# Row numbers loaded four at a time, row loads three quads ahead, early sums regrouped in DRAM, z rows by plain gathers

## The chip, the cores and the metric

The kernel runs on one core of a Trainium2 chip. The core has TensorE (PE), VectorE (DVE), ScalarE (ACT), GpSimd (POOL) and SyncE (SP). Of these SP, ACT and POOL issue transfers here, and all transfers share 16 DMA engines. The metric is the device time of one execution in microseconds (us); lower is better.

## The reference, cut to what matters

```python
N, E, D, F = 12500, 212500, 256, 128
h = relu(layernorm(x))                                # (N, D)
in_deg  = min(segment_sum(1, dst, N), 511)
out_deg = min(segment_sum(1, src, N), 511)
sum3d   = segment_sum(edge_attr @ W_sum + b_sum, src, N)   # edge_attr is (E, F)
cent = sigmoid(centralities @ W_cent + b_cent)
vor  = sigmoid(voronoi_values @ W_vor + b_vor)
out = x + h + z_in[in_deg] + z_out[out_deg] + cent + vor + sum3d
```

The edges come in order of `dst`, and the heavy part is the sum over `src`, which is random. Everything is float32.

## The kernel before, in words

Node `100 a + w` belongs to window `w` (100 windows) and lies on partition `a` (125 partitions). A tile is 128 edges, a quad four tiles; there are 416 quads, cut into four segments of 25, 175, 130 and 86 quads. Within a segment the kernel sorts edge rows by window with a counting sort into DRAM, then reads the sorted rows back and adds them up.

The sort, for quad `q` (all engines run one loop over quads, each with its own written order of instructions):

- SP loads edge rows into `edge_ring`, six slots of five tiles (L354 to L359). A slot is refilled when its scatters have landed; SP asks for that at quad `q` for scatters of about quad `q - 4` (`LOAD_AHEAD`, L384 to L386).
- DVE makes the one-hot tile `hot_w` of the next quad (L517), PE ranks it against running counts (`rank`, L870), ACT reduces the ranks to positions (`positions`, L762) and writes each edge's key behind its row (`row_keys`, L769), PE adds the quad to the counts (`rebase`, L876 and L877, behind the quad's pieces in PE's order), and DVE turns positions into indices (`index`, L703, the last thing of its quad). `INDEX_RING` is 12 quads deep: DVE waits for the scatters of quad `q - 12`.
- POOL scatters each tile's 128 rows of 520 bytes to the segment's area in DRAM (L427), one indirect DMA a tile.

A segment's sorted rows are read back during the next segment, in pieces of 256 rows, one window each: 150, 450, 360 and 270 pieces (one piece for each 256 rows and one for each window). For piece `n`: its issuer waits for slot `n % 11` of `piece_ring`, reads the row number from `row_i` into a register (L343, a TENSOR_LOAD, then FUSED_REGOPS and SEQ_ASSERT for the bounds) and issues the load of 130 KB (L344, with one FUSED_REGOPS and one MOVE ahead); DVE makes the one-hot matrix `hot_n` (L585); PE multiplies (L886, four matmul records, two row groups of two passes); DVE folds the product onto the sum of the window so far in `stage` (L608), six stages of two pieces; ACT stores two pieces' sums at a time to `sums` in DRAM (L777). `sums` has 125 partitions, 1230 pieces and 129 numbers (128 sums and the count). `last_i` tells which piece holds a window's whole sum.

A planner at the head (L110 to L164) lays out `side[q]`, the list of side work of quad `q` that every engine walks: it spreads the pieces of the segment before evenly over the quads from `quad0[s] + LAG` (`LAG = INDEX_RING + 2`) to four quads before the segment's end, and puts node work (sigmoids, layernorm, ACT and DVE), histogram work for the in-degrees and others where a cost table leaves room under `BUDGET`. In the main loop SP issues a quad's piece loads at that quad (L391 to L393), behind its edge load.

The last segment's 270 pieces come behind the main loop, in one loop over `c` on each engine. SP loads the even pieces, ACT the odd ones (ten ahead). POOL gathers the z_in rows of all windows into `base` with an accumulating indirect DMA (L434). From `c = 170 + 10` on, window `w = c - 180` is finished: four rows of `sums`, one for each segment, are loaded into `table_ring` (six slots; SP the first two segments, ACT the other two; for each one register read at L330 and one load at L331, 63 KB in 125 partitions of 516 bytes); four steps later DVE adds the four counts (L676), makes `out_i` (L678), adds count times b_sum (L683), POOL gathers the z_out row with accumulation (L434), PE transposes and adds the four tables (L897, eight matmul records), ACT copies (L791), PE multiplies by W_sum (L907), and DVE adds to `base` (L689). SP stores `base` to the output behind its loop (L403).

## Time and profile before

| What | us |
|---|---|
| median of 3 runs | 3323.89 |
| lowest and highest run | 3298.01, 3340.47 |
| the profiled execution's own time | 3312.39 |
| its span in the trace | 3310.5 |

```profile
PE 2012.2 (61%) x9285; PEld 1456.0 (44%) x9285; DVE 1798.8 (54%) x5794; ACT 762.6 (23%) x3965; POOL 2067.2 (62%) x1869
```

The line gives each engine's busy time, its share of the span and its instructions. PEld is TensorE's load of weights. SP has no row, as it only issues. The page cuts the span in 40 slices of 83 us, a digit being tenths:

```profile
PE   6546766776443366676666636666665666466664
DVE  8646677777346556666666645454544445233331
POOL 4777777777777776566666674444446885344443
PEclk8656666666555577777777657667776556677786
DMA  3346644544554377777777647677775997555558
```

PEclk is the granted TensorE clock in tenths of full speed, DMA the mean busy share of the 16 DMA engines. Times in the text are from the span's start. An engine name with q behind it (SPq, ACTq) is the engine's queue: waits, register work and issues of transfers.

### The profile page before, as it was taken

Reading aid. Unit: us, or ns where it says so; the run is one execution under the profiler, and the core shown is the slowest. Engines: PE = TensorE matmul, PEld = TensorE weight load, DVE = VectorE, ACT = ScalarE, POOL = GpSimd, SP = SyncE. Lnnn points to the kernel's source line nnn. Section 1 sums busy time; section 2 is a strip of 40 time slices with the busy share of each in tenths; the row PEclk is TensorE's granted clock in tenths of the full one; section 3 lists DMA queues with packets and bytes.
Section 4 is the critical chain, followed back from the end, with each engine's and each line's share of the span. In section 5 each row is a group of like instructions: output and inputs, shape, how many; then the busy total and the mean of one; then the engine's idle time right before and its main releaser. Section 6 shows DMA issues by size and latency. Waiting matters only on the chain.

```text
span 3310.5 us, 47321 instructions
## 1 busy us (share of the span) xinstructions
PE 2012.2 (61%) x9285; PEld 1456.0 (44%) x9285; DVE 1798.8 (54%) x5794; ACT 762.6 (23%) x3965; POOL 2067.2 (62%) x1869
## 2 busy tenths in 40 slices
PE   6546766776443366676666636666665666466664
PEld 2235544444221045455555415555553555455553
DVE  8646677777346556666666645454544445233331
ACT  2222322222245422222233341111111000000000
POOL 4777777777777776566666674444446885344443
PEclk8656666666555577777777657667776556677786
DMA  3346644544554377777777647677775997555558
GB/s 106 102 142 195 186 135 133 140 136 133 145 143 122 103 204 203 201 209 207 207 216 214 184 127 192 187 192 191 195 196 154 188 187 174 130 123 130 128 129 212
DMA packets 671281, 546.20 MB, mean 165 GB/s; under 512 B 116444, under 2 KB 639549, under 8 KB 670990
## 3 DMA queue, kind: packets, MB, share of 16 engines
q1 hardware_dynamic: 409188, 296.29, 33.3%
q0 software_dynamic: 136352, 136.66, 17.9%
q10 hardware_dynamic: 125450, 110.23, 11.1%
q8 instruction: 78, 1.28, 0.2%
q14 instruction: 213, 1.74, 0.2%
HBM read 339.32 MB, written 203.17 MB: 164 GB/s over the span
## 4 chain that ended last, share of the span: by engine, by line
DMA 27%; POOL 24%; issue 13%; PE 12%; SPq 9%; ACTq 7%; DVE 6%; ACT 1%; DVEq 0%; POOLq 0%
POOL sorted L427 24%; DMA piece_ring<-sorted 24%; PE bank L886 9%; SPq L343 5%; ACTq L330 3%; DVE hot_n L585 2%; ACTq L331 2%; SPq L344 2%; DMA sums<-stage 1%; PE bank L897 1%; DMA sorted<-edge_ring,pos_i 1%; ACTq L343 1%; PE bank L907 1%; DVE gate L646 1%; SPq L357 0%
## 5 line engine op out<-in xcount | busy, mean ns | idle before, releaser
L427 POOL DMA_INDIRECT sorted<-edge_ring,pos_i x1660 | 1664.9, 1003 | 880.0 <-issue 449.8
L886 PE MATMUL bank<-piece_ring,hot_n 128*125 128x129 f32 x4920 | 1120.3, 385 | 863.3 <-DVE hot_n L585 859.3
L886 PEld LDWEIGHTS bank<-piece_ring,hot_n 128*125 128x125 f32 x4920 | 932.1, 272 | 1127.1 <-DVE hot_n L585 1104.2
L585 DVE SCALAR_TENSOR_TENSOR hot_n<-bank,wkey,piece_ring 128x250 f32<-128x250 f32 x1230 | 583.7, 475 | 1180.6 <-DMA piece_ring<-sorted 1139.3
L762 ACT ACTIVATE junk<-bank,mark_col 128x100 bf16<-128x100 f32 x1664 | 549.7, 342 | 1401.9 <-PE bank L870 1386.9
L608 DVE SCALAR_TENSOR_TENSOR stage<-stage,same,bank 125x129 f32<-125x129 f32 x1226 | 417.4, 340 | 106.1 <-DMA sums<-stage 91.1
L434 POOL DMA_INDIRECT base<-in_L_gnn_z_out_dram,out_i x100 | 199.5, 1995 | 305.2 <-DVE base L689 213.5
L762 ACT ACTIVATION_READ_ACCUMULATOR junk<-bank,mark_col 128x1 f32 x1664 | 337.4, 203 | 0.0
L876 PE MATMUL bank<-hot_w,after_b 128*128 128x400 bf16 x416 | 192.2, 462 | 171.5 <-ACT junk L762 171.5
L913 PE MATMUL bank<-hot_dl,hot_dh 128*125 128x100 bf16 x1661 | 224.9, 285 | 36.6 <-DVE hot_dh L517 36.1
L913 PEld LDWEIGHTS bank<-hot_dl,hot_dh 128*125 128x125 bf16 x1661 | 186.4, 191 | 86.7 <-DVE hot_dh L517 69.3
L434 POOL DMA_INDIRECT base<-in_L_gnn_z_in_dram,deg_i x100 | 199.4, 1994 | 30.6 <-issue 30.6
L870 PE MATMUL bank<-hot_w,before_b 128*128 128x400 bf16 x416 | 191.1, 459 | 4.5 <-DVE hot_w L517 4.5
L791 ACT ACTIVATE sumT<-bank 128x125 f32<-128x125 f32 x100 | 27.6, 277 | 720.1 <-DVE stage L608 311.0
L877 PE MATMUL bank<-hot_w,unmark_b 128*128 128x400 bf16 x416 | 193.0, 464 | 0.0
L841 PE MATMUL bank<-hot_t,ones_b 128*128 128x400 bf16 x416 | 155.3, 417 | 46.0 <-DVE hot_t L517 45.5
L907 PE MATMUL bank<-w_sb,sumT 128*125 128x256 f32 x200 | 91.2, 547 | 131.8 <-ACT sumT L791 116.0
L517 DVE TENSOR_TENSOR hot_dh<-dst_parts,iota_h 128x500 bf16<-128x500 bf16 x416 | 171.1, 411 | 0.0
L517 DVE TENSOR_TENSOR hot_w<-src_w,iota_h 128x400 bf16<-128x400 bf16 x416 | 148.7, 358 | 0.0
L876 PEld LDWEIGHTS bank<-hot_w,after_b 128*128 128x128 bf16 x416 | 53.9, 130 | 213.1 <-ACT junk L762 212.3
L897 PEld LDWEIGHTS bank<-ident,edge_ring 125*128 125x128 f32 x800 | 142.7, 251 | 10.6
L517 DVE TENSOR_TENSOR hot_dl<-dst_parts,iota_h 128x400 bf16<-128x400 bf16 x416 | 147.3, 354 | 0.1
(102 smaller groups left out, 1247.6 us busy)
## 6 DMA issues: line engine op xcount, KB each, us to landing
piece_ring<-sorted SPq DMA_DIRECT2D x1095, 130.0 KB, 3.9
edge_ring<-in_edge_attr_dram SPq DMA_DIRECT2D x332, 320.0 KB, 3.8
sums<-stage ACTq DMA_DIRECT2D x615, 126.0 KB
sorted<-edge_ring,pos_i POOLq DMA_INDIRECT x1660
piece_ring<-sorted ACTq DMA_DIRECT2D x135, 130.0 KB, 6.4
edge_ring<-sums SPq DMA_DIRECT2D x200, 63.0 KB
edge_ring<-sums ACTq DMA_DIRECT2D x200, 63.0 KB
base<-in_x_dram SPq DMA_DIRECT2D x20, 560.0 KB
```

The source lines that it names most:

```text
L343: row = eng.value_load(row_i[32 * (s % 2):32 * (s % 2) + 1, c:c + 1], min_val=0, max_val=edges_in[s])
L427: g.indirect_dma_start(rows, bass.IndirectOffsetOnAxis(index, 0), edge_ring[:, slot, at, :], None).then_inc(s_scatter[slot], 16)
L434: g.indirect_dma_start(base[0:NODE_P, w, :], None, table[:, :], bass.IndirectOffsetOnAxis(index[0:NODE_P, w:w + 1], 0), compute_op=ALU.add ...
L517: return v.tensor_tensor(to, part.unsqueeze(2).to_broadcast([P, 2, n, 2]), iota_h[:, 0:n, :].unsqueeze(1).to_broadcast([P, 2, n, 2]), ALU. ...
L585: v.scalar_tensor_tensor(out=hot_n[:, n % HOT_SLOTS, 0:G, :], in0=iota_ps.unsqueeze(1).to_broadcast([P, G, LOC]), scalar=wkey[:, s % 2, c: ...
L608: v.scalar_tensor_tensor(out=to, in0=stage[0:LOC, (n - 1) // STAGE % STAGES, (n - 1) % STAGE, :], scalar=same[0:LOC, s % 2, c:c + 1], in1=new,
L762: last = a.activation(junk[:, t, :], part[:, t // 2, :, t % 2], ACT.Relu, bias=mark_col[:, :], accum_out=pos_f[:, q % 4, t:t + 1])
L870: t_.matmul(ps_rank, before_b[:, :], hot, start=False, stop=True, skip_group_check=True).then_inc(s_rank, 1)
L876: t_.matmul(ps_rank, after_b[:, :], hot, start=False, stop=False, skip_group_check=True)
L877: t_.matmul(ps_rank, unmark_b[:, :], hot, start=False, stop=True, skip_group_check=True).then_inc(s_based, 1)
L886: last = t_.matmul(to, hot_n[:, n % HOT_SLOTS, k, :], piece_ring[:, n % PIECE_SLOTS, k, 0:SUM], start=(k == 0), stop=(k == ROW_GROUPS[s] - 1))
L913: last = t_.matmul(ps_in_count, hot_dh[:, b, t // 2, :, t % 2], hot_dl[:, b, t // 2, :, t % 2], start=(h == 0 and t == 0), stop=(h == NQ - ...
```

## The change

- Row numbers and table numbers are read four at a time into registers (`ROWS_LOADED = 4`); the bounds work and the issue stay one for each. `last_i` is laid out by segment, so that four windows lie side by side.
- In the main loop SP issues the piece loads of quad `q + 3` at quad `q` (`PIECE_AHEAD = 3`). The other engines keep `side[q]`.
- `INDEX_RING` is 8 for 12, so `LAG` is 10 for 14, and pieces are spread until three quads before the segment's end. `BUDGET` is 5.1 for 5.0.
- SP issues all the last segment's piece loads; ACT none.
- New side work "early": in segments 2 and 3, for the first and second segment, ACT copies each window's sums from `sums` to `early_sums` (window, segment and numbers side by side), DRAM to DRAM, four windows an item, 25 items a segment. In the tail SP loads three windows of both segments with one transfer into `early_ring` (two slots, over `key_f`). `table_ring` holds the two later segments, eight slots; SP loads one, ACT the other.
- z rows are gathered without accumulation into `z_rows`, six slots over `dst_parts`, and DVE adds them: z_in at steps 20 to 119 of the last loop, z_out ahead of the product's addition.

```diff
-AHEAD = 10
-TABLE_SLOTS = 6
+PIECE_AHEAD = 3
+ROWS_LOADED = 4
+TABLE_SLOTS = 8
+EARLY = 2
+EARLY_WINDOWS = 3
-Z_GROUP = 10
-INDEX_RING = 12
+INDEX_RING = 8
+Z_LAG = 20
+EARLY_LAG = LOAD_LAG + 2
-BUDGET = 5.0
+BUDGET = 5.1
...
+    early_sums = nc.dram_tensor("early_sums", (NODE_P, SW, EARLY, SUM), F32).ap()
+            "early": [(s + 2, ("early", s, w)) for s in range(EARLY) for w in range(0, SW, ROWS_LOADED)],
...
-            for _ in range(min(-(-len(left) // max(1, quad0[s + 1] - 4 - q)), len(left))):
+            for _ in range(min(-(-len(left) // max(1, quad0[s + 1] - 3 - q)), len(left))):
+        left = [x for x in todo["early"] if x[0] == s]
+        if left and q >= quad0[s]:
+            every = max(1, (quad0[s + 1] - 2 - quad0[s]) // (SW // ROWS_LOADED))
+            if (q - quad0[s]) % every == 0 or q >= quad0[s + 1] - 2:
+                put(q, todo["early"].pop(0)[1])
...
+        def loaded(engine, ap, top):
+            return nc.values_load_multi_w_load_instructions(ap, engines=[engine], min_val=0, max_val=top)[1]
...
+            def load(self, c):
+                eng, s = self.eng, self.s
+                n = piece0[s] + c
...
+                if c % ROWS_LOADED == 0:
+                    self.values = loaded(self.engine, row_i[32 * (s % 2):32 * (s % 2) + 1,
+                                                            c:min(c + ROWS_LOADED, pieces[s])], edges_in[s])
+                if n >= PIECE_SLOTS:
+                    eng.wait_ge(s_piece, n - PIECE_SLOTS + 1)
+                row = self.values[c % ROWS_LOADED]
+                eng.dma_start(piece_ring[:, n % PIECE_SLOTS, 0:ROW_GROUPS[s], :].rearrange("p k f -> p (k f)"),
...
-                for what, s, i in side[q] + (after if q == NQ - 1 else []):
+                for what, s, i in side_ahead[q]:
                     if what == "piece":
-                        load_piece(sp, s, i)
+                        rows[s].load(i)
+            sp.wait_ge(s_row_key, NLOAD + 1)
+            sp.wait_ge(s_early_out, 16 * EARLY * SW)
             ahead = pieces[NS - 1] - SW
-            for c in range(pieces[NS - 1] + LOAD_LAG):
-                if c < pieces[NS - 1] and c % 2 == 0:
-                    load_piece(sp, NS - 1, c)
-                if c >= ahead + LOAD_LAG:
-                    load_tables(sp, c - ahead - LOAD_LAG, range(NS // 2))
+            for c in range(pieces[NS - 1] + EARLY_LAG):
+                if c < pieces[NS - 1]:
+                    rows[NS - 1].load(c)
+                if c >= ahead + EARLY_LAG and c - ahead - EARLY_LAG in early_start[:-1]:
+                    load_early(early_start.index(c - ahead - EARLY_LAG))
+                if ahead + LOAD_LAG <= c < pieces[NS - 1] + LOAD_LAG:
+                    tables.load(c - ahead - LOAD_LAG)
...
+                if n >= GATHERS:
+                    pool.wait_ge(s_z_in_added, min(n - GATHERS + 1, NW))
+                if n >= NW + GATHERS:
+                    pool.wait_ge(s_added, n - NW - GATHERS + 1)
+                g.indirect_dma_start(z_rows[0:NODE_P, n % GATHERS, :], None, table[:, :],
+                                     bass.IndirectOffsetOnAxis(index[0:NODE_P, w:w + 1], 0)
+                                     ).then_inc(s_z_row[n % GATHERS], 16)
...
+            def add_z(n):
+                acc = base[0:NODE_P, n % NW, :]
+                dve.wait_ge(s_z_row[n % GATHERS], 16 * (n // GATHERS + 1))
+                return v.tensor_tensor(acc, z_rows[0:NODE_P, n % GATHERS, :], acc, ALU.add)
...
+            def copy_early(s, w0):
+                wait_sums(act, piece0[s + 1])
+                for w, at in enumerate(loaded(mybir.EngineType.Activation, last_i[0:1, s, w0:w0 + ROWS_LOADED],
+                                              piece0[NS] - 1), w0):
+                    act.dma_start(early_sums[:, w, s, :], sums[:, bass.ds(at, 1), :].rearrange("p o f -> p (o f)")
+                                  ).then_inc(s_early_out, 16)
...
-            for c in range(1, AHEAD, 2):
-                load_piece(act, NS - 1, c)
...
-                if c + AHEAD < pieces[NS - 1] and (c + AHEAD) % 2 == 1:
-                    load_piece(act, NS - 1, c + AHEAD)
```

## Rows read from the trace of the kernel before

**Rows 1.** Windows; busy us of PE, PEld, DVE, ACT, POOL, PEclk, DMA, GB/s.
```profile
200.00:1100.00 900.00, 536.81 (x2752) 354.40 (x2750) 546.86 (x1886) 285.04 (x1546) 693.63 (x678) 0.61 0.51 146
1172.00:1867.00 695.00, 478.57 (x2156) 352.62 (x2156) 448.34 (x1385) 212.73 (x1050) 432.86 (x444) 0.74 0.76 210
...
1990.00:2530.00 540.00, 356.25 (x1578) 279.11 (x1577) 269.60 (x824) 98.64 (x581) 252.59 (x265) 0.71 0.71 192
2548.00:2820.00 272.00, 169.73 (x728) 144.09 (x728) 132.12 (x362) 0.00 (x0) 200.38 (x102) 0.61 0.86 180
2820.00:3255.00 435.00, 265.66 (x1298) 227.94 (x1298) 151.36 (x557) 25.73 (x93) 189.16 (x95) 0.76 0.58 128
3255.00:3311.00 56.00, 15.93 (x55) 13.19 (x54) 6.20 (x22) 1.82 (x7) 10.29 (x6) 0.57 0.89 256
```

**Rows 2.** Groups, 1172 to 1867 us; busy, mean ns, idle before, releasers.
```profile
L427 POOL DMA_INDIRECT sorted<-edge_ring,pos_i x444 | 432.9, 975 | 262.1 <-DVE pos_i L703 149.6 <-issue 110.7 <-ACT edge_ring L769 1.8
...
L585 DVE SCALAR_TENSOR_TENSOR hot_n<-bank,wkey,piece_ring 128x250 f32<-128x250 f32 x439 | 208.4, 475 | 242.1 <-DMA piece_ring<-sorted 239.2 <-PE bank L886 1.3
...
L762 ACT ACTIVATE junk<-bank,mark_col 128x100 bf16<-128x100 f32 x439 | 144.9, 342 | 330.2 <-PE bank L870 323.2 <-DVE stage L608 7.0
```

**Rows 3.** Groups of instructions from 1990 to 2530 us.
```profile
L427 POOL DMA_INDIRECT sorted<-edge_ring,pos_i x265 | 253.8, 958 | 287.7 <-DVE pos_i L703 226.7 <-issue 59.8 <-ACT edge_ring L769 1.2
L585 DVE SCALAR_TENSOR_TENSOR hot_n<-bank,wkey,piece_ring 128x250 f32<-128x250 f32 x344 | 163.6, 475 | 263.2 <-DMA piece_ring<-sorted 262.2
```

**Rows 4.** Timeline of SyncE's queue from 1430 us; start, duration, instruction.
```profile
1430.65 5.17 SPq L344 DMA_DIRECT2D piece_ring<-sorted  x4
1435.87 0.43 SPq L357 DMA_DIRECT2D edge_ring<-in_edge_attr_dram  x1
1437.07 4.36 SPq L344 DMA_DIRECT2D piece_ring<-sorted  x4
```

**Rows 5.** Lines 343 and 344, 1172:1867; ns least/median/most, landing in us.
```profile
L343 SPq TENSOR_LOAD <-row_i x440: 262/412/2368, 1171.8 to 1866.9; - x147
L343 SPq FUSED_REGOPS  x439: 152/152/159, 1172.5 to 1866.1; - x147
...
L344 SPq DMA_DIRECT2D piece_ring<-sorted x439: 332/333/711, 1172.9 to 1866.5; - x147
...
DMA to landing us min/median/max: 2.1/4.1/5.6
```

**Rows 6.** Waits from 2548 to 2820 us; us in total, times, longest.
```profile
DVE stage L608 <- DMA sums<-stage: 91.1, 73, 3.2
DVE hot_n L585 <- DMA piece_ring<-sorted: 49.5, 47, 18.9
```

**Rows 7.** Line 344 from 2548 to 2820 us.
```profile
DMA to landing us min/median/max: 2.9/6.6/9.9
```

**Rows 8.** Chain of waits from 3003 us; start us, us, what.
```profile
3002.54 0.69 ACTq L330
...
3003.63 0.51 ACTq L331
...
3004.17 0.47 ACTq L330
...
3005.03 0.51 ACTq L331
```

**Rows 9.** Line 344 from 200 to 1000 us.
```profile
DMA to landing us min/median/max: 2.6/3.0/4.7
```

**Rows 10.** Line 434, the gathers of z rows; ns least/median/most.
```profile
L434 POOL DMA_INDIRECT base<-in_L_gnn_z_in_dram,deg_i x100: 1982/1992/2054, 2549.6 to 2777.3; - x100
```

**Rows 11.** Groups of instructions from 2820 to 3255 us.
```profile
L689 DVE TENSOR_TENSOR base<-bank,base 125x256 f32<-125x256 f32 x91 | 37.9, 417 | 3.1 <-DMA base<-in_L_gnn_z_out_dram,out_i 3.1
```

**Rows 12.** Line 343 from 2560 to 2740 us.
```profile
L343 SPq TENSOR_LOAD <-row_i x61: 270/795/2391, 2560.8 to 2737.4; - x61
```

**Rows 13.** Line 344 from 2880 to 3200 us.
```profile
DMA to landing us min/median/max: 4.0/4.6/5.7
```

More of the change, by code:

```diff
@@ L162, in gnn_kernel @@
                     break
-    assert not todo["totals"] and not todo["stats"]
+    assert not todo["totals"] and not todo["stats"] and not todo["early"]
     after = [x[1] for kind in ("piece", "hist", "node") for x in todo[kind]]
+    side_ahead = [side[q] for q in range(PIECE_AHEAD, NQ)]
+    side_ahead = [sum(side[0:PIECE_AHEAD + 1], [])] + side_ahead[1:] + [after] + [[] for _ in range(PIECE_AHEAD - 1)]
+    assert len(side_ahead) == NQ
     store_start = list(range(0, SW, STORE_WINDOWS)) + [SW]
@@ L257, in gnn_kernel @@
         s_table_in = [sem(f"s_table_in{i}") for i in range(TABLE_SLOTS)]
-        s_z_in = [sem(f"s_z_in{i}") for i in range(NW // Z_GROUP)]
-        s_z_out = [sem(f"s_z_out{i}") for i in range(GATHERS)]
+        s_early_out = sem("s_early_out")
+        s_early_in = [sem(f"s_early_in{i}") for i in range(2)]
+        s_z_row = [sem(f"s_z_row{i}") for i in range(GATHERS)]
+        s_z_in_added = sem("s_z_in_added")
         s_out = sem("s_out")
@@ new lines, in gnn_kernel, with __init__, load @@
+        class Tables:
+            def __init__(self, eng, engine, s):
+                self.eng, self.engine, self.s, self.values = eng, engine, s, []
+            def load(self, w):
+                eng, s, slot = self.eng, self.s, w % TABLE_SLOTS
+                if w == 0:
+                    wait_scattered(eng, NT)
+                if w % ROWS_LOADED == 0:
+                    self.values = loaded(self.engine, last_i[0:1, s, w:w + ROWS_LOADED], piece0[NS] - 1)
+                if w >= TABLE_SLOTS:
+                    eng.wait_ge(s_sumT, w - TABLE_SLOTS + 1)
+                    eng.wait_ge(s_out_deg, w - TABLE_SLOTS + 1)
+                wait_sums(eng, piece0[s] + edges_in[s] // rows_in[s] + w + 1)
+                at = self.values[w % ROWS_LOADED]
+                eng.dma_start(table_ring[0:NODE_P, slot, s - EARLY, :],
+                              sums[:, bass.ds(at, 1), :].rearrange("p o f -> p (o f)")).then_inc(s_table_in[slot], 16)
@@ L380, in x_windows, with load_early @@
                     sp.dma_start(base[p0:p1, w0:w1, :], by_partition(x)[p0:p1, w0:w1, :]).then_inc(s_x[i], 16)
+            def load_early(g):
+                w0, w1 = early_start[g:g + 2]
+                if g >= 2:
+                    sp.wait_ge(s_sumT, early_start[g - 1])
+                    sp.wait_ge(s_out_deg, early_start[g - 1])
+                sp.dma_start(early_ring[0:NODE_P, g % 2, 0:w1 - w0, :, :].rearrange("p w s n -> p (w s n)"),
+                             early_sums[:, w0:w1, :, :].rearrange("p w s n -> p (w s n)")
+                             ).then_inc(s_early_in[g % 2], 16)
+            rows = [Rows(sp, mybir.EngineType.SP, s) for s in range(NS)]
+            tables = Tables(sp, mybir.EngineType.SP, EARLY)
             X0 = quad0[1] + 4
@@ L816, in _ @@
                         a.activation(gate[0:NODE_P, b, :], gate[0:NODE_P, b, :], ACT.Sigmoid).then_inc(s_gate, 1)
+                    elif what == "early":
+                        copy_early(s, i)
                     elif what == "piece":
@@ L827, in _ @@
                 if ahead + LOAD_LAG <= c < pieces[NS - 1] + LOAD_LAG:
-                    load_tables(act, c - ahead - LOAD_LAG, range(NS // 2, NS))
+                    tables.load(c - ahead - LOAD_LAG)
                 if c >= ahead + SUM_LAG + 1:
```

99 lines of the change are left out of this document (49 added, 50 removed).

## The prediction

> **What bounds the kernel now.** I read the table of windows first, then the pieces of each stage, SyncE's queue, the waits and the chain. A quad is four tiles of 128 edges.
>
> Until about 1110 us GpSimd's scatters set the pace: 678 of them in 900 us, busy 693.6 us [rows 1], each followed by a gap of 0.3 us, so 1.33 us each, 5.3 us a quad. Nothing of the change lies there.
>
> From 1172 to 1867 us 444 scatters pass in 695 us, 111 quads at 6.26 us; from 1990 to 2530 us 265 in 540 us, 66 quads at 8.15 us [rows 1]. A scatter still takes 975 and 958 ns [rows 2, 3], so with its gap GpSimd could do a quad in 5.05 us; it now waits for VectorE's index (149.6 and 226.7 us), which stands behind pieces whose rows have not landed (239.2 and 262.2 us) [rows 2, 3]. In both stages a piece comes every 1.57 us (439 in 695, 344 in 540) [rows 2, 3]: the same, though a quad has 4 in one and 5.2 in the other. That is the mark of a queue that works one piece after another. SyncE's queue shows it: four pieces, an edge load, four pieces again, 6.42 us from turn to turn [rows 4]. Per piece it has the read of the row number (least 262, median 412 ns, but up to 2368), 0.152 of register work and 0.333 for the issue [rows 5]; with three small ones (0.08) and six gaps of some 0.05 that is 0.84 us beside the read. 1.57 us, less 0.1 us for a share of the edge loads, leaves 0.63 us as the mean read. Four pieces and an edge load (0.43) make 6.3 us, the turn seen. The sum closes, so SyncE's issue is the bound of both stages.
>
> From 2548 to 2820 us, with 180 of the last segment's pieces, it is 1.51 us a piece; the DMA share is 0.86 [rows 1], VectorE waits for stores of sums, 91.1 us, and rows, 49.5 us [rows 6], and row loads land in 6.6 us [rows 7]. Transfers bind; the accumulating gathers of z_in run here.
>
> From 2820 to 3255 us, 100 windows at 4.35 us: the chain goes through ScalarE's queue for whole windows: read 0.69 and 0.47, register work, issue 0.51 twice, then the copy, then the same again [rows 8]. From read to read a table load takes 1.63 us; the copy, and every other window a piece load of about 1.5, fill the 4.35. The last 56 us [rows 1] are the stores of the output.
>
> **The change part by part.**
>
> *Four numbers per read.* It takes three of four reads. SyncE then needs 0.84 + 0.63/4 = 1.0 us a piece if a read of four costs as one; if it costs four times as much nothing is gained (1.47). I take 1.05, since reads of 262 ns at the least [rows 5] are likely one round trip. Nothing in the trace shows a read of four. The Trainium skill ("DMA: Bandwidth & Descriptors", Latency and other measured facts) gives such a load a floor of about 600 ns and says that compilers unroll it four times to spread it; the trace shows 262 ns as the least, so the floor does not hold here, and with it the sum would be 0.99 instead of 1.0.
>
> *Three quads ahead, spread wider.* 450 pieces now go over 117 quads (3.85 each, was 112) and 360 over 73 (4.93, was 68). SyncE needs 3.85 x 1.05 + 0.4 = 4.4 us and 5.6 us a quad. Behind it stand GpSimd at 5.05; DMA, 0.76 x 6.26 = 4.8 and 0.71 x 8.15 = 5.8 us of full engines a quad [rows 1]; PE 478.6/111 = 4.3 and 356/66 = 5.4 us; VectorE about 4.0 in both. Fewer pieces a quad take 4% and 7% off, the early copies add 0.8 and 1.3 transfers of 63 KB a quad, some 5%. The first stage's floor is so 5.05, its ceiling today's 6.26: I take 5.65, since GpSimd and DMA are both near and loads already land later (4.1 us) [rows 5] than in the quiet stretch (3.0) [rows 9]. The second: floor 5.8, and at the DMA share of 0.86 that the trace has reached over a long stage 6.7; ceiling 8.15. I take 6.8. Eleven quads fewer lie outside these stages, each 5.4 us. Sum: 111 and 68 quads cost 695 + 554 = 1249 now; afterwards 661 + 496 = 1157, and the eleven quads less elsewhere give 59: gain **150 us**.
>
> *Early copies.* Fifty batches on ScalarE of four copies: 4 x (0.16 + 0.152 + 0.51 + 0.3 small) = 4.5 us, with waits 5.3. ScalarE is busy 212.7 of 695 us [rows 1] and waits 323 us for PE [rows 2]; positions of the next quad are wanted only behind its pieces on PE. I take zero; uncovered it is 265 us (rival below). A gain is excluded here, it comes in the tail.
>
> *Plain gathers.* An accumulating gather takes 1992 ns on GpSimd [rows 10], a plain scatter 975 [rows 2]; I take 1.0 (bounds 0.9 to 2.0). What it takes off the DMA engines no row shows; I count it in the ranges below. Added: VectorE's addition, 0.42 us by its like [rows 11], 200 times.
>
> *The last segment's first 180 pieces.* SyncE alone now: reads are slow here (median 795 ns) [rows 12], so 0.84 + 0.25 = 1.1 us. VectorE 0.475 + 0.34 + 0.42 = 1.24 us while z_in is added (100 pieces), 0.85 after. DMA 0.86 x 1.51 = 1.3 us, less with plain gathers. Taken: 1.3 x 100 + 1.0 x 80 = 210 us (bounds 195 and 290) for 272: gain **62 us**.
>
> *The 100 table windows.* SyncE: piece 1.05, table 0.15 + 0.15 + 0.29 + 0.35 and waits 0.35, a third of an early load 0.2: 2.55 us. ScalarE: table 1.3 + waits, half a store, the copy: 2.2. VectorE 151.4/100 + 0.42 + 0.15 = 2.1. GpSimd 1.3. PE 265.7 us for 100 windows, 2.7 at a granted clock of 0.76 [rows 1]. DMA 0.58 x 4.35 = 2.5. Floor 2.7, ceiling 4.35; each engine's order is fixed and four of them lie within a microsecond, so I take 3.6: gain **75 us**. The output stores begin when SyncE leaves its loop, as now: 56 us unchanged.
>
> Sum: 150 + 62 + 75 = 287; 3312.4 of the profiled execution less 287 = 3025. The median of the three runs is 11 us above that execution, so **3035 us**.
>
> **The rivals.**
>
> *Transfers of 125 partitions fill their engines (chance 0.18).* Sums' stores, table loads and the early copies have 125 rows; if they run on few of the 16 engines, a mean share of 0.76 can hide full ones. For: landings grow from 3.0 to 4.1 us, and tail windows with a share of only 0.58 show 4.6 [rows 5, 9, 13]. Against: at saturation they were 6.6 [rows 7]. Then the sort stages keep today's pace per piece: 0 of 150, and the tail half: 3312 - 62 - 37 = 3213, by the median 3225 us. The Trainium skill ("DMA: Bandwidth & Descriptors", Why a DMA increments its semaphore by 16 and not by 1) says that the engine count is the largest k up to 16 that divides the slowest dimension: 5 for 125. The rows do not name engines, so they neither confirm nor deny it.
>
> *The read of four costs four reads (0.10).* SyncE stays at 1.5 us a piece: 3.85 x 1.5 + 0.4 = 6.2, 4.93 x 1.5 + 0.4 = 7.8 us a quad: 725 + 569 less 59, a gain of 14; the 180 pieces, now on one queue at 1.7, cost 306, a loss of 34; tail +60. 3312 - 40 = 3272, by the median 3283 us. For: the read's mean rises with the traffic, so it may cost by the word. Against: the least is 262 ns for a whole read, so a word more need not cost as much.
>
> *The early batches stop ScalarE (0.10), the slower side.* Each batch holds the queue 5.3 us, and a store of sums behind it lands 4.1 us later; VectorE's fold waits for stores (it did for 91 us [rows 6]), then index, then scatter. 50 x 9.4 = 470: 3025 + 470 = 3495, by the median 3505 us. It turns the result slower from 287/50 = 5.7 us a batch. Against: ScalarE's idle time, and six stages of stores.
>
> **How the numbers follow.** Forecast 0.62, rivals 0.18, 0.10, 0.10. The likeliest's own range is 2880 to 3150: all floors at once (5.1, 5.9, 195 us, 2.7) would give 2800, all ceilings the rivals' times. With the first rival the range is **2860 to 3235**. A measurement of this kernel tells about 2% from no change. Faster by over 2% (below 3257): 0.62 + 0.14 + 0.04 = 0.80; within 2%: 0.11; slower: 0.09.
>
> **What would show it.** One read for four issues on SyncE; pieces in the two sort stages every 1.45 and 1.4 us; GpSimd's scatters close to back to back in the first; VectorE's wait for rows well under half; gathers at 1.0 us; windows at 3.6 us with PE, no longer ScalarE's queue, in the chain. Wrong, if the scatter pace stays at 6.2 us with landings over 6 us, if folds wait for stores after each batch, or if a read of four takes over 1.5 us.

## The result, and the profile after

| What | us |
|---|---|
| median of 3 runs | 3165.5 |
| the profiled execution's own time | 3167.5 |
| its span in the trace | 3165.7 |
| ratio to the kernel before | 0.9534, interval 0.9435 to 0.9633 |

The change takes 145 us off the profiled execution (3312.4 to 3167.5), where 287 were forecast, and 158 us off the median (3323.89 to 3165.5), for which 3035 us were forecast. The table of windows of the kernel after, cut where the same stages begin and end (columns as in [rows 1]):

```profile
200.00:1125.00 925.00, 557.20 (x2754) 360.88 (x2754) 554.04 (x1897) 295.52 (x1568) 715.89 (x686) 0.60 0.50 143
1197.00:1841.00 644.00, 414.85 (x2073) 310.79 (x2074) 450.80 (x1409) 225.45 (x1078) 444.55 (x449) 0.80 0.81 230
...
1935.00:2409.00 474.00, 285.00 (x1499) 230.31 (x1498) 249.56 (x781) 102.39 (x587) 258.12 (x269) 0.77 0.78 221
2428.00:2661.00 233.00, 160.91 (x718) 134.55 (x719) 157.75 (x458) 0.00 (x0) 123.12 (x102) 0.68 0.76 209
2661.00:3108.00 447.00, 253.60 (x1272) 228.13 (x1272) 208.82 (x732) 25.02 (x91) 110.91 (x93) 0.74 0.43 122
3108.00:3166.00 58.00, 17.73 (x94) 14.89 (x92) 14.91 (x51) 2.57 (x10) 8.83 (x8) 0.65 0.81 266
```

GpSimd's scatters count the quads, so like can be set beside like:

| Stage | before, us | after, us | change |
|---|---|---|---|
| up to the scatters of quad 200 | 1109 | 1125 | +16 |
| quad 200 to the last scatter | 1439 | 1304 | -135 |
| of it quads 214 to 326 (first sort stage) | 703 (6.28 a quad) | 644 (5.75) | -59 |
| of it quads 344 to 411 (second) | 545 (8.14) | 474 (7.08) | -71 |
| the last segment's 180 pieces | 266 | 233 | -33 |
| from there to the end | 497 | 504 | +7 |
| of it 89 table windows | 406 (4.56 a window) | 424 (4.76) | +18 |

So the sort stages and the 180 pieces gain, and the table windows, from which 75 us were to come, lose 18. In the first sort stage, by groups of instructions:

```profile
L487 POOL DMA_INDIRECT sorted<-edge_ring,pos_i x449 | 445.5, 992 | 199.8 <-issue 123.8 <-DVE pos_i L777 72.1 <-ACT edge_ring L845 3.8
L647 DVE SCALAR_TENSOR_TENSOR hot_n<-bank,wkey,piece_ring 128x250 f32<-128x250 f32 x418 | 197.4, 472 | 0.1
L670 DVE SCALAR_TENSOR_TENSOR stage<-stage,same,bank 125x129 f32<-125x129 f32 x420 | 144.3, 343 | 74.0 <-DMA sums<-stage 64.7 <-PE bank L969 4.6
```

VectorE's wait for rows, 239.2 us in [rows 2], is gone: earlier issue and the faster queue together have removed it. GpSimd's wait for the index falls from 149.6 to 72.1 us, but the scatters are still not back to back: 199.8 us idle, 262.1 before. A new wait stands in the fold, 64.7 us for stores of sums. What SyncE does now, the reads at line 347 and then its waits, both in the same stage:

```profile
L347 SPq FUSED_REGOPS  x406: 147/152/159, 1201.4 to 1814.6; - x136
...
L347 SPq TENSOR_LOAD <-row_i x102: 296/432/2232, 1201.1 to 1813.8; - x102
```

```profile
SPq L368 <- PE bank L969: 160.6, 72, 6.8
```

102 reads serve 406 pieces, each 432 ns at the median, against 412 for one number [rows 5]. SyncE's queue now stands for a free piece slot. Such a row has to be checked: the same view of the kernel before puts 97.7 us of line 343 down to PE, yet matched piece by piece the slot had been free for over 8 us in nine loads of ten; a later piece's increment of the same semaphore fell into the read. In the kernel after it is real: two to three loads in ten are issued within 0.2 to 0.4 us after PE freed their slot. In the second stage the groups show where the wait has moved:

```profile
L487 POOL DMA_INDIRECT sorted<-edge_ring,pos_i x269 | 259.2, 964 | 216.2 <-DVE pos_i L777 124.2 <-issue 67.5 <-ACT edge_ring L845 24.6
L647 DVE SCALAR_TENSOR_TENSOR hot_n<-bank,wkey,piece_ring 128x250 f32<-128x250 f32 x325 | 153.5, 472 | 4.9 <-DMA piece_ring<-sorted 4.7
L670 DVE SCALAR_TENSOR_TENSOR stage<-stage,same,bank 125x129 f32<-125x129 f32 x324 | 111.7, 345 | 106.4 <-DMA sums<-stage 96.8 <-PE bank L969 6.9 <-issue 0.2
L838 ACT ACTIVATE junk<-bank,mark_col 128x100 bf16<-128x100 f32 x267 | 88.1, 342 | 267.8 <-DMA sums<-stage 134.4 <-PE bank L953 64.8 <-issue 48.7
```

The waits of that stage also have ScalarE standing for edges:

```profile
ACT edge_ring L845 <- DMA edge_ring<-in_edge_attr_dram: 112.3, 24, 8.3
```

ScalarE, which had neither wait in this stage before, waits 134.4 us for stores of sums and 112.3 us for edge loads; from it come the positions and from them the index. In the tail, SyncE's timeline over one turn (line 432 is an early load, 389 a table load, 368 a piece load):

```profile
2807.03 0.30 SPq L432 DMA_DIRECT2D key_f<-early_sums  x1
2809.41 0.30 SPq L389 DMA_DIRECT2D edge_ring<-sums  x1
2809.92 0.37 SPq L368 DMA_DIRECT2D piece_ring<-sorted  x1
...
2811.19 0.36 SPq L368 DMA_DIRECT2D piece_ring<-sorted  x1
...
2812.45 0.39 SPq L368 DMA_DIRECT2D piece_ring<-sorted  x1
2821.25 0.26 SPq L432 DMA_DIRECT2D key_f<-early_sums  x1
```

And VectorE's pieces beside it, with the idle time before each in brackets:

```profile
2801.52 0.48 DVE L647 SCALAR_TENSOR_TENSOR hot_n<-bank,wkey,piece_ring 128x250 f32<-128x250 f32 x1 [6.94 <-DMA piece_ring<-sorted]
2803.88 0.47 DVE L647 SCALAR_TENSOR_TENSOR hot_n<-bank,wkey,piece_ring 128x250 f32<-128x250 f32 x1
2806.24 0.47 DVE L647 SCALAR_TENSOR_TENSOR hot_n<-bank,wkey,piece_ring 128x250 f32<-128x250 f32 x1
2815.73 0.48 DVE L647 SCALAR_TENSOR_TENSOR hot_n<-bank,wkey,piece_ring 128x250 f32<-128x250 f32 x1 [7.05 <-DMA piece_ring<-sorted]
```

The turn is 14.2 us for three windows, half of it a hole: pieces go at 2.36 us, then VectorE idles 7.05 us for rows. The rows of the piece at 2815.73 were issued at 2809.92; before that SyncE's queue stood. Its waits between 2661 and 3108 us say at what:

```profile
SPq L432 <- PE bank L984: 121.2, 30, 4.2
SPq L431 <- DVE out_i L752: 112.7, 30, 4.9
```

Lines 431 and 432 are the early load's wait for a slot of its ring, which has two: the load of group g waits for the last window of group g-2, and the next piece load stands behind it in the same queue.

### The profile page after: what moved, and what is told of

It is laid out like the page before. It is cut to its first block and busy times, and to the rows that moved or that the text cites. A ratio compares the mean times of both kernels' runs of the same rounds, so it can differ in the third digit from the quotient of the medians.

```text
span 3165.7 us, 46745 instructions
## 1 busy us (share of the span) xinstructions
PE 1904.0 (60%) x9285; PEld 1391.7 (44%) x9285; DVE 1879.5 (59%) x6094; ACT 771.6 (24%) x3965; POOL 1933.8 (61%) x1869
## 5 line engine op out<-in xcount | busy, mean ns | idle before, releaser
L487 POOL DMA_INDIRECT sorted<-edge_ring,pos_i x1660 | 1689.2, 1018 | 736.4 <-issue 467.3
L969 PE MATMUL bank<-piece_ring,hot_n 128*125 128x129 f32 x4920 | 1017.5, 363 | 459.9 <-DVE hot_n L647 455.6
L969 PEld LDWEIGHTS bank<-piece_ring,hot_n 128*125 128x125 f32 x4920 | 873.3, 257 | 656.4 <-DVE hot_n L647 619.8
L777 DVE CAST pos_i<-pos_f 128x4 int32<-128x4 f32 x416 | 80.6, 194 | 543.7 <-ACT junk L838 532.4
L500 POOL DMA_INDIRECT dst_parts<-in_L_gnn_z_out_dram,out_i x100 | 119.7, 1197 | 408.3 <-DVE out_i L752 408.3
L959 PEld LDWEIGHTS bank<-hot_w,after_b 128*128 128x128 bf16 x416 | 47.4, 114 | 692.6 <-ACT junk L838 691.6
L845 ACT ACTIVATE edge_ring<-key_f 128x5 f32<-128x5 f32 x332 | 70.9, 214 | 926.4 <-DMA edge_ring<-in_edge_attr_dram 925.5
L500 POOL DMA_INDIRECT dst_parts<-in_L_gnn_z_in_dram,deg_i x100 | 121.5, 1215 | 48.0 <-DVE base L739 24.4
```

The costliest lines, as they stand in the source:

```text
L487: g.indirect_dma_start(rows, bass.IndirectOffsetOnAxis(index, 0), edge_ring[:, slot, at, :], None).then_inc(s_scatter[slot], 16)
L500: g.indirect_dma_start(z_rows[0:NODE_P, n % GATHERS, :], None, table[:, :], bass.IndirectOffsetOnAxis(index[0:NODE_P, w:w + 1], 0)).then_i ...
L959: t_.matmul(ps_rank, after_b[:, :], hot, start=False, stop=False, skip_group_check=True)
L969: last = t_.matmul(to, hot_n[:, n % HOT_SLOTS, k, :], piece_ring[:, n % PIECE_SLOTS, k, 0:SUM], start=(k == 0), stop=(k == ROW_GROUPS[s] - 1))
```

## The experiments

The experiments ran on four other chips than the two kernels above. The kernel before was timed on each of them: 3609 us on the chip of `e1` to `e4`, 3614 on that of `e5` to `e8`, 3628 on that of `e9` to `e11` and 3664 on that of `e12_before`, where the first chip gave 3324. The ratios in the table are each taken on the run's own chip. The stages are read against `e12_before` and `e5_after`, and that crosses chips: `e12_before` ran on the slowest, so a difference against its row holds up to 36 to 55 us that belong to the chip. Against `e5_after` the chips differ by 5 to 14 us.

The diffs below show each edit's main lines and leave out what stands between them. The table gives medians of the timed runs, and per stage what counting scatters and pieces in each trace gives. The stages are as above, but the 180 pieces are counted from the first of them and not from the last scatter, which takes 5 to 8 us off.

| Run | us | ratio to before | quad 200 to last scatter | first, second stage, us a quad | 180 pieces | us a window |
|---|---|---|---|---|---|---|
| e12_before | 3665 | 1.0015 | 1632 | 7.41, 8.69 | 260 | 4.45 |
| e5_after | 3529 | 0.9748 | 1534 | 6.91, 7.94 | 223 | 4.74 |
| e4_before_read4 | 3475 | 0.9596 | 1442 | 6.76, 7.09 | 259 | 4.70 |
| e2_read1 | 3629 | 1.0065 | 1590 | 7.08, 8.47 | 259 | 4.78 |
| e3_ahead0 | 3478 | 0.9614 | 1474 | 6.85, 7.07 | 223 | 4.75 |
| e6_no_early | 3410 | 0.9417 | 1474 | 6.77, 7.32 | 226 | 4.00 |
| e1_ring6 | 3438 | 0.9516 | 1520 | 6.86, 7.84 | 229 | 3.78 |
| e7_rows128_ring6 | 3273 | 0.9046 | 1480 | 6.79, 7.38 | 218 | 2.64 |
| e8_accumulate | 3572 | 0.9886 | 1515 | 6.82, 7.85 | 238 | 5.04 |
| e9_before_rows128 | 3483 | 0.9611 | 1516 | 7.01, 7.74 | 243 | 4.05 |
| e10_rows128_ring6_ahead0 | 3253 | 0.8978 | 1456 | 6.78, 7.04 | 216 | 2.67 |
| e11_rows128_no_early_ahead0 | 3302 | 0.9115 | 1430 | 6.72, 6.78 | 219 | 3.34 |

**e5_after and e12_before**, the two kernels unchanged, as the measure.

> The changed kernel as it is, run again beside the others of this call, as their measure: ratio 0.94 to 0.97 to the kernel before, table windows at 4.7 to 4.8 us.

> The kernel before, profiled beside the experiments, as the measure of their stages. Theory A (SyncE's issue bounds both sort stages here too): a piece every 1.55 to 1.75 us, so 6.7 to 7.3 and 8.2 to 8.6 us a quad, windows 4.4 to 4.7 us, row reads of 0.6 us in the mean. Rival B (something else bounds the sort stages on these chips): the time of a piece differs by more than 10% between the two stages.

The kernel after takes 3529.01 us there, ratio 0.9748 (0.9667 to 0.9828): the change is worth less on these chips, and by intervals that do not overlap. As the interval reaches past 0.98, it is not certain there that the gain is over 2%. The kernel before, windows of both stages with its scatters:

```profile
1363.00:2193.00 830.00, 436.94 (x448) 0.67 0.65 179
2307.00:2889.00 582.00, 256.42 (x268) 0.66 0.67 182
```

A scatter is as long as on the first chip (975 and 957 ns, [rows 2, 3]), yet the first stage takes 7.41 us a quad. With 445 and 354 pieces in these windows SyncE's pace is 1.87 and 1.64 us a piece, no longer the same in both: on these chips more than its issue holds the first stage, as rival B of `e12_before` had it. Part of it can be counted in the traces: SyncE's queue has holes of over 0.3 us between instructions that wait for nothing, 177 us of them in the first stage of `e12_before` and 83 us in the second, against 7 us in the first stage on the first chip. Before quad 200 GpSimd waits 182.5 us for the index, against 40.7 on the first chip. What makes the holes stays open. The windows cost the same as on the first chip (4.45 and 4.56; after 4.74 and 4.76), so what is found in the tail should hold on the first chip too.

**e4_before_read4**: the kernel before with only the reads of four.

```diff
-            row = eng.value_load(row_i[32 * (s % 2):32 * (s % 2) + 1, c:c + 1], min_val=0, max_val=edges_in[s])
+                if c % ROWS_LOADED == 0:
+                    values[s] = nc.values_load_multi_w_load_instructions(
+                        row_i[32 * (s % 2):32 * (s % 2) + 1, c:min(c + ROWS_LOADED, pieces[s])],
+                        engines=[mybir.EngineType.SP], min_val=0, max_val=edges_in[s])[1]
+                row = values[s][c % ROWS_LOADED]
```

> The kernel before with only one part of the change: in the main loop the row numbers of pieces are read four at a time. Theory A (issue of SyncE was the bound of both sort stages, 1.57 us a piece): the first stage goes from 6.28 to 5.3 to 5.9 us a quad, the second from 8.1 to 7.0 to 7.6 us, so 60 to 150 us less, ratio 0.955 to 0.98. Rival B (five full DMA engines were the bound): ratio 0.99 to 1.0.

0.9596 (0.9522 to 0.9669), 135 us below before on the same chip, so rival B has fallen. Its second stage, 67 quads, with the scatters (before: the second line above, 582 us for the same 268):

```profile
2209.00:2684.00 475.00, 256.46 (x268) 0.78 0.78 223
```

8.69 to 7.09 us a quad: SyncE's issue was the bound there, and reading four at once lifts it. By the table the sort stages lose 190 us, of which up to 55 can be the chip of `e12_before`. This one edit leaves them at 1442 us, and the whole change at 1534.

**e2_read1**: the whole change, but one number read per piece.

```diff
-                if c % ROWS_LOADED == 0:
-                    self.values = loaded(self.engine, row_i[32 * (s % 2):32 * (s % 2) + 1,
-                                                            c:min(c + ROWS_LOADED, pieces[s])], edges_in[s])
-                row = self.values[c % ROWS_LOADED]
+                row = loaded(self.engine, row_i[32 * (s % 2):32 * (s % 2) + 1, c:c + 1], edges_in[s])[0]
```

> The changed kernel with the row numbers of pieces read one at a time again (tables still four at a time). Theory A (SyncE's issue is no longer the bound, but reads of one bring it back): 1.5 us a piece on SyncE, the sort stage 6.1 us a quad for 5.75 and 7.7 for 7.1 us, 234 us of the 180 pieces to 270: 3250 to 3290 us. Rival B (the gain of the two sort stages came from the wider spread and the earlier issue): 3165 to 3200 us.

1.0065 (1.0029 to 1.0102): without the reads of four nothing of the gain is left. Against `e5_after` the second stage goes back from 7.94 to 8.47 and the 180 pieces from 223 to 259 us. That is theory A. The rival "the read of four costs four reads" has fallen.

**e3_ahead0**: the change with no lead.

```diff
-PIECE_AHEAD = 3
+PIECE_AHEAD = 0
-    side_ahead = [sum(side[0:PIECE_AHEAD + 1], [])] + side_ahead[1:] + [after] + [[] for _ in range(PIECE_AHEAD - 1)]
+    side_ahead = [sum(side[0:PIECE_AHEAD + 1], [])] + side_ahead[1:-1] + [side_ahead[-1] + after]
```

> The changed kernel with the piece loads issued at their own quad (0 ahead for 3). Theory A (SyncE is faster than the pieces, so without the lead VectorE waits for each quad's first rows): sort stages 6.0 and 7.3 us a quad, 3190 to 3240 us. Rival B (three quads ahead makes SyncE stand at the piece slots, and the edge loads behind it come late, so that ScalarE waits for edges 248 us in the two stages): without the lead that wait goes and the time falls to 3100 to 3150 us.

3477.67 us, 51 less than `e5_after`, as rival B had it. The two ran on different chips, but no run of one comes within 39 us of a run of the other, and the kernel before differs by 5 us between these chips. Nearly all of it is in the second stage. The windows of the scatters there, first `e5_after`:

```profile
2240.00:2772.00 532.00, 257.26 (x269) 0.76 0.72 201
```

then `e3_ahead0`, one scatter fewer:

```profile
2237.00:2711.00 474.00, 256.55 (x268) 0.78 0.78 225
```

The waits of `e5_after` in that window have the edge loads:

```profile
ACT edge_ring L845 <- DMA edge_ring<-in_edge_attr_dram: 108.5, 25, 9.9
```

The list of `e3_ahead0` has no such wait. Its VectorE waits 68.1 us for rows, where `e5_after` has 3.0: the lead does what it was made for, and still costs. That edge loads come late with it can be counted: SyncE issues an edge load 41.5 us (median) after the last scatter of its slot in `e5_after` and 17.6 us after it in `e3_ahead0`, and the first scatter of the loaded rows follows the issue by 11.0 and 27.1 us. The queue is in order, so an edge load stands behind the piece loads of three more quads. What is not shown is that waits for piece slots make it late. That fits the kernel after on the first chip, where SyncE waits 122.9 us for slots in this stage, but in `e5_after` it waits 11.6 us, and about one piece load in twenty is issued right after its slot came free.

**e6_no_early**: no early copies; all four segments of a window through the table ring, which gets seven slots; segments 0 and 1 on SyncE, 2 and 3 on ScalarE.

```diff
-TABLE_SLOTS = 8
+TABLE_SLOTS = 7
-            "early": [(s + 2, ("early", s, w)) for s in range(EARLY) for w in range(0, SW, ROWS_LOADED)],
+            "early": [],
-        LATE = NS - EARLY
+        LATE = NS
-            tables = Tables(sp, mybir.EngineType.SP, EARLY)
+            tables = [Tables(sp, mybir.EngineType.SP, s) for s in (0, 1)]
```

> The changed kernel without the early copies: the tail loads four rows of sums a window as before (SyncE the first two segments, ScalarE the others, four numbers a read), seven slots. Theory A (the copies cost in the sort stages, by ScalarE's queue and by traffic, and in the tail the early ring costs more than it saves): sort stages 30 to 80 us shorter and windows at 3.7 to 4.3 us, so 60 to 170 us less than the changed kernel run beside it. Rival B (the early copies carry the change's gain in the tail): windows at 4.9 us or more, 0 to 60 us more.

3410.44 us, 119 less than `e5_after`: 60 in the sort stages (1534 to 1474), and 4.00 for 4.74 us a window, 66 us over 89 windows. So the copies cost on both sides, where they were made and where they were to pay, as theory A had it. Whether they cost by holding ScalarE's queue or by their traffic the run does not separate.

**e1_ring6**: the early ring with six slots of one window, where there were two of three windows: the same space, waits for window w-6.

```diff
-EARLY_WINDOWS = 3
+EARLY_WINDOWS = 1
+EARLY_RING = 6
-                if g >= 2:
-                    sp.wait_ge(s_sumT, early_start[g - 1])
+                if g >= EARLY_RING:
+                    sp.wait_ge(s_sumT, early_start[g - EARLY_RING + 1])
```

> The changed kernel with the early sums loaded one window at a time into six slots, instead of three windows at a time into two slots; the space is the same. Theory A (SyncE stands at the early load until the group two before is used up, which is the window two steps back, and the row loads of the next pieces stand behind it; each three windows then cost one round trip of about 14 us): the wait goes back to four steps, the hole of 7 us in front of every third piece goes, and a table window falls from 4.76 us to 3.0 to 3.8 us, so 95 to 175 us less, 2990 to 3070 us. Rival B (the five engines that carry transfers of 125 partitions are full in the tail): the same bytes pass, a window stays at 4.5 to 4.8 us, within 25 us of 3165.

3437.66 us, 91 less than `e5_after`. SyncE's waits over the windows, all that is left of the two lines above:

```profile
SPq L433 <- PE bank L985: 2.5, 7, 0.8
```

VectorE's pieces of the tail in `e5_after`, and below it in `e1_ring6`:

```profile
L647 DVE SCALAR_TENSOR_TENSOR hot_n<-bank,wkey,piece_ring 128x250 f32<-128x250 f32 x89 | 42.0, 472 | 219.6 <-DMA piece_ring<-sorted 219.6
```

```profile
L648 DVE SCALAR_TENSOR_TENSOR hot_n<-bank,wkey,piece_ring 128x250 f32<-128x250 f32 x89 | 42.5, 478 | 128.2 <-DMA piece_ring<-sorted 128.1
```

Of the 219.6 us wait for rows 91 go, the same 91 that the kernel gains. A window costs 3.78 us, within theory A, while the gain falls just short of its 95 to 175 us. The hole was the ring's wait. 128 us of waiting for rows are left. Now SyncE's queue hardly ever stands: it has 6 us of holes over 0.3 us in the 336 us, and its issues take long. Line 369 is the piece load:

```profile
L369 SPq DMA_DIRECT2D piece_ring<-sorted x89: 344/405/2823, 3018.1 to 3346.5; - x89
```

**e7_rows128_ring6**: e1 with the sums, their stores and both kinds of table loads over 128 rows in place of 125; the three more are zeros, set once.

```diff
-    sums = nc.dram_tensor("sums", (NODE_P, piece0[NS], SUM), F32).ap()
+    sums = nc.dram_tensor("sums", (P, piece0[NS], SUM), F32).ap()
-                act.dma_start(sums[:, n0:n0 + STAGE, :], stage[0:LOC, b, :, :]).then_inc(s_sum_out[b], 16)
+                act.dma_start(sums[:, n0:n0 + STAGE, :], stage[:, b, :, :]).then_inc(s_sum_out[b], 16)
-                eng.dma_start(table_ring[0:NODE_P, slot, s - EARLY, :],
+                eng.dma_start(table_ring[:, slot, s - EARLY, :],
```

> The changed kernel with six single early windows, and with 128 rows instead of 125 in sums and early_sums, so that their stores, copies and loads have 128 partitions (three rows are filler). Theory A (transfers of 125 rows run on 5 of the 16 engines, and these are near full in sort stages and tail): the same bytes on 16 engines; stores land sooner, VectorE's 168 us and ScalarE's 241 us of waits for them nearly go, sort stages 5.2 to 5.5 and 6.0 to 6.6 us a quad, windows 3.2 to 3.7 us: 60 to 160 us less than with six windows alone. Rival B (the mean DMA share is what counts): within 25 us of it.

3273.0 us, ratio 0.9046, 165 less than `e1_ring6` and 256 less than `e5_after`. The windows of the tail with VectorE's pieces, `e5_after`, `e1_ring6` and `e7_rows128_ring6` in turn:

```profile
3026.00:3448.00 422.00, 42.05 (x89) 0.73 0.43 122
```

```profile
3018.00:3354.00 336.00, 42.50 (x89) 0.84 0.53 154
```

```profile
2966.00:3202.00 236.00, 42.11 (x89) 0.96 0.85 222
```

The same 89 windows take 422, 336 and 236 us. Rival B, the mean DMA share, has fallen: with 125 rows transfers held the stage at a mean share of 0.53, and with 128 rows it reaches 0.85 and 222 GB/s. How they held it shows in SyncE's queue. In `e7_rows128_ring6` the same issue is shorter:

```profile
L369 SPq DMA_DIRECT2D piece_ring<-sorted x89: 5/333/1054, 2966.7 to 3198.5; - x89
```

By the mean its issue falls from 976 to 346 ns, and that of SyncE's table load from 751 to 288 ns. That is 1.09 us a window, of the 1.14 us that a window loses. So with 125 rows SyncE's issue still ended last, and its length was set by the transfers. VectorE's wait for rows falls on:

```profile
L649 DVE SCALAR_TENSOR_TENSOR hot_n<-bank,wkey,piece_ring 128x250 f32<-128x250 f32 x89 | 42.1, 473 | 31.8 <-DMA piece_ring<-sorted 28.4 <-issue 3.1
```

In the sort stages the same edit is worth 40 us (1520 to 1480); at 6.79 and 7.38 us a quad they stay far from the 5.2 to 5.5 and 6.0 to 6.6 expected. There the reads of numbers get quicker, also on ScalarE, whose reads have no slot wait in them. First stage, line 348 of `e1_ring6`, then of `e7_rows128_ring6` (`e5_after`, on the chip of the latter, has a median of 1554 ns, so it is not the chip):

```profile
L348 ACTq TENSOR_LOAD <-last_i x22: 494/1433/2448, 1350.0 to 2070.3; - x22
```

```profile
L348 ACTq TENSOR_LOAD <-last_i x22: 307/320/635, 1349.8 to 2062.9; - x22
```

The Trainium skill ("DMA: Bandwidth & Descriptors", Why a DMA increments its semaphore by 16 and not by 1) states that a transfer runs on as many engines as the largest divisor up to 16 of its slowest dimension, 5 for 125 and 16 for 128. No row here names engines, but the time agrees with it: 3.78 to 2.64 us a window for three rows more.

**e9_before_rows128**: the kernel before, with that edit alone.

```diff
-                eng.dma_start(table_ring[0:NODE_P, w % TABLE_SLOTS, s, :],
+                eng.dma_start(table_ring[:, w % TABLE_SLOTS, s, :],
```

> The kernel before with one thing changed: sums has 128 rows for 125, so that stores of sums and table loads have 128 partitions. Theory A (before, issue on SyncE bounds the sort stages and ScalarE's queue the table windows; full DMA engines come only after those are gone): ratio 0.98 to 1.0, windows 4.2 to 4.6 us. Rival B (the engines that carry 125-row transfers were already a bound before): sort stages under 6.0 and 7.7 us a quad, windows under 4.0, ratio below 0.96.

0.9611 (0.9558 to 0.9665), 145 us below the kernel before on the same chip. Theory A (0.98 to 1.0) has fallen, and rival B is not met either, though narrowly in three of its four numbers: 0.9611 for below 0.96, 7.01 and 7.74 us a quad for under 6.0 and 7.7, 4.05 us a window for under 4.0. Most of the gain is in the sort stages, 1632 to 1516, though up to 36 us of that can be the chip. The row reads (line 343) tell how. In the second stage, first of `e12_before`, then of `e9_before_rows128`:

```profile
L343 SPq TENSOR_LOAD <-row_i x351: 3/275/1890, 2307.2 to 2882.8; - x176
```

```profile
L343 SPq TENSOR_LOAD <-row_i x351: 3/268/732, 2236.8 to 2749.1; - x176
```

The medians are alike, but the longest falls from 1890 to 732 ns and the mean of these 351 records from 470 to 269 ns; in both kernels the slots had long been free. The chip is not the reason: `e2_read1`, with 125 rows on a third chip, has a mean of 483 ns in this stage. So a read takes longer while 125-row transfers run beside it, and SyncE pays for it at every piece: 0.2 us by 5.3 pieces is 1.06 us a quad, and the stage went from 8.69 to 7.74. Two different edits, reading less often and making reads quicker, ease the same bound.

**e8_accumulate**: the z rows added by the gathers again, in base, with no addition on VectorE.

```diff
-                g.indirect_dma_start(z_rows[0:NODE_P, n % GATHERS, :], None, table[:, :],
-                                     bass.IndirectOffsetOnAxis(index[0:NODE_P, w:w + 1], 0)
+                g.indirect_dma_start(base[0:NODE_P, w, :], None, table[:, :],
+                                     bass.IndirectOffsetOnAxis(index[0:NODE_P, w:w + 1], 0), compute_op=ALU.add
```

> The changed kernel with the z rows gathered by accumulating transfers into base again, VectorE's additions of z left out. Theory A (accumulation is dear for the DMA engines, 118 to 127 ns a packet of 1 KB against some 55): the 180 pieces go from 234 us to 260 to 290 us, the windows stay at 4.7 to 5.0: 25 to 70 us more than the changed kernel run beside it. Rival B (VectorE's additions cost as much as they save): within 15 us.

3572.2 us, 43 more than `e5_after`, within theory A, though the 180 pieces give 15 us of it and not 26 or more. Its windows of the 180 pieces and of the tail:

```profile
2789.00:3027.00 238.00, 84.85 (x180) 0.63 0.91 198
3027.00:3476.00 449.00, 42.28 (x90) 0.71 0.53 117
```

A share of 0.91 for 198 GB/s in the 180 pieces, against 0.77 for 215 in the 223 us of `e5_after`: the accumulating gathers load the DMA engines more for less. Plain gathers are worth 15 us in the 180 pieces and 0.3 us a window. The second is not the price of the transfer alone, since accumulating in `base` also makes each gather wait for the bias and VectorE's last addition wait for the gather.

**e10_rows128_ring6_ahead0** and **e11_rows128_no_early_ahead0** put the findings together: e7 with no lead, and the same without the early copies.

> Six single early windows, 128 rows, and piece loads issued at their own quad. Theory A (the lead makes SyncE stand at the slots and the edge loads behind it come late; taking it away gave 50 us in the second sort stage): 30 to 60 us less than the same with a lead of three, ratio 0.885 to 0.90. Rival B (with 128 rows slots come free sooner, so that the lead costs nothing): ratio 0.90 to 0.91.

> No early copies, 128 rows, piece loads at their own quad; tail with two table loads a window on SyncE and two on ScalarE. Theory A (the early copies still hold ScalarE 5 us a batch, but save a load and a number a window in the tail): sort stages 20 to 50 us shorter than with copies, windows 3.2 to 3.5 us for 2.6, so 10 to 60 us more than with them, ratio 0.89 to 0.915. Rival B (with 16 engines behind them four loads a window are hidden): windows under 3.0 us and a ratio below 0.885, the fastest of all.

`e10` is the best version: 3253.03 us, 0.8978 (0.8925 to 0.903), faster than both kernels. It is 20 us below `e7_rows128_ring6`, less than the 30 to 60 expected, and the intervals of the two ratios overlap, so what the lead still costs with 128 rows is small and not settled. `e11` comes to 0.9115. Its sort stages are the fastest of all (1430), but a window costs 3.34 against 2.67 us, as theory A had it: once their ring and their rows are mended, the copies pay, 60 us over 89 windows for 26 in the sort stages.

## Why the prediction was right or wrong

The direction and the range held (2860 to 3235; 3165.5 measured), the size did not: 142 of the 287 us were missing, 31 in the sort stages, 29 in the 180 pieces and 82 behind them. The range was wide enough for that because it held the first rival, and not because the windows were understood. Term by term, on the first chip unless a run is named:

- **SyncE's issue is the bound of the sort stages.** Right. VectorE's wait for rows went from 239.2 to 0.1 us, and the reads of four alone give 0.9596 (`e4_before_read4`). What the prediction did not see is that the length of a read, a term of this issue, hangs on the shape of other transfers (`e9_before_rows128`).
- **A read of four costs one read.** Right: 432 against 412 ns at the median, 624 against 635 in the mean. The 1.05 us a piece could not be seen as a pace, since SyncE now waits for slots.
- **Sort stages, gain 150.** 119 measured up to the last scatter: 59 and 71 in the two stages where 0.61 and 1.35 us a quad were forecast (68 and 92), and a loss of 16 before quad 200 that nothing in the prediction has. 13 us of that loss lie between quads 40 and 100, where 22 scatters take over 1.3 us, against 4 in the kernel before; the gaps between scatters are the same (73 us). On the experiments' chips it is the kernel before that is slower up to quad 200 (1278 us in `e12_before`, 1262 in `e5_after`), so no run ties the loss to the change. The forecast put the lead into one term with the wider spread, which comes from `LAG` and not from it, and gave it no cost; it costs 51 us (`e3_ahead0`).
- **Early copies, zero in the sort stages.** Wrong in this step: "ScalarE's idle time" does not cover them whole. A copy was priced at 0.51 us of issue, as a table load; line 868 of the kernel after shows

```profile
L868 ACTq DMA_DIRECT2D early_sums<-sums x200: 692/1156/4204, 1099.9 to 2362.3; - x100
```

  so four of them with their small ones take 4 x (0.16 + 0.15 + 1.16 + 0.3) = 7.1 us and not 4.5. That is not the whole reason: on the experiments' chips the median is 0.70 us, which makes 5.2 us a batch, and yet taking the copies away gives 60 us in the sort stages there (`e6_no_early`). With 128 rows and no lead it gives 26. Of the third rival's 470 us an eighth or less has come; whether by its mechanism, stores held up behind a batch, or by traffic stays open.
- **The 180 pieces, gain 62.** 33 measured. The gathers were taken at 1.0 us and are longer, in line 500's row:

```profile
L500 POOL DMA_INDIRECT dst_parts<-in_L_gnn_z_in_dram,deg_i x100: 1192/1198/1443, 2430.2 to 2598.2; - x100
```

  With the gap of 0.3 us, 100 of them are 150 us, 20 more than the 130 taken for these pieces, and VectorE waits for their rows 42.5 us. VectorE's addition was right (0.423 us).
- **The table windows, gain 75.** This step failed, and is the largest miss: a window took 4.76 us in place of 3.6, and was 4.56 before. The sum over each engine's own work was made with a wait of 0.35 us on SyncE, and the early load's condition was not followed: a ring of two groups ties SyncE's queue to work of the group two before, with the piece loads behind it. That the orders are fixed was written down, but not what each waiting instruction has behind it. With six slots a window takes 3.78 us (`e1_ring6`). That this is close to 3.6 is luck: SyncE's issues, priced at about 0.35 us, took 0.98 and 0.75 us in the mean there, and with 128 rows a window takes 2.64, at the floor of 2.7 that the sum of work had given.
- **Transfers of 125 partitions fill their engines (0.18).** Borne out in the tail by time (`e7_rows128_ring6`), though no row names engines: a mean share of 0.43 to 0.58 was read as half idle. The row that spoke for it [rows 13], landings of 4.6 us at a share of 0.58 [rows 1], weighed more than the prediction gave it. In the sort stages 125-row transfers cost in a way not foreseen, through slow reads of row numbers. This rival's time did not come: it had the sort stages keep their pace, and reading four at once alone changed it.
- **The output stores unchanged.** Right: 58 us.

## What to carry to other kernels

When a queue's own issue is the bound, batch the register reads first; other parts of such a change are worth measuring one at a time, since here taking out the lead gave 51 us and taking out the copies 119. A prefetch with its own ring in a queue that also feeds the critical path must have slots enough that its wait never ends last: ask of each wait what stands behind it. A mean DMA share of 0.53 was no sign of free engines here, with transfers of 125 rows; look at how long the issues in a queue take, and try the padding, since three rows more took 165 us off.

## What the runs showed of the hardware that was not expected

- Register reads from SBUF depend on the shape of other transfers: mean 470 ns with 125-row tables and sums and 269 ns with 128 rows on SyncE (`e12_before`, `e9_before_rows128`), median 1433 and 320 ns on ScalarE (`e1_ring6`, `e7_rows128_ring6`).
- So does the issue of a transfer: a piece load holds SyncE's queue 976 ns in the mean in the tail of `e1_ring6` and 346 ns in that of `e7_rows128_ring6`, though the piece load itself has 128 rows in both.
- A copy of 125 rows from DRAM to DRAM holds ScalarE's queue 1.16 us at the median and up to 4.2 us in the kernel after, and 0.70 us in `e5_after`; with 128 rows it is 0.50 us (`e7_rows128_ring6`). SyncE issues a piece load in 0.333 us.
- The granted clock was 0.96 in the tail of `e7_rows128_ring6`, nearly all of it at the higher level of 2.4 GHz; PE was busy 179 of 236 us there. It was 0.74 in the tail of the kernel after, a mix of both levels, with PE busy 254 of 447 us. A matmul of a piece took 290 and 375 ns in these stages:

```profile
L971 PE MATMUL bank<-piece_ring,hot_n 128*125 128x129 f32 x360 | 59.3, 290 | 8.8 <-DVE hot_n L649 8.8
```

```profile
L969 PE MATMUL bank<-piece_ring,hot_n 128*125 128x129 f32 x364 | 84.8, 375 | 159.7 <-DVE hot_n L647 159.7
```

- Chips differ: the same kernel took 3324 us on one and 3609 to 3664 us on four others. In the trace of the slowest all of the difference lies before the last scatter (2911 against 2549 us). The same edit was worth 0.9534 on one and 0.9748 on another.
